# Feed-forward products in three 16-bit products, with downward products laced between upward ones

## The reference

```python
x = x + gnn(layernorm(x), src, dst, ...)
x = x + ffn(layernorm(x)[None], ...)[0]
# ffn: one batch of N = 6250 rows, D = 256, F = 512, E = 8 experts, 2 chosen for the whole batch
h   = gelu(einsum('nd,edf->enf', xf, W1) + b1[:, None, :], approximate=False)
y   = einsum('enf,efd->end', h, W2) + b2[:, None, :]
out = einsum('ne,end->nd', w_dense, y)          # w_dense: weights of the two chosen experts
out = layer_norm(out + x, gamma, beta)
```

## Time and profile before

| | |
|---|---|
| time, median of 3 runs | 3208.35 us (3207.71 to 3212.56) |
| the profiled execution | 3210.56 us, span of its trace 3208.6 us |
| PE busy | 3076.7 us (96%) |
| DVE busy | 1901.3 us (59%) |
| ACT busy | 855.9 us (27%) |
| POOL busy | 70.3 us (2%) |
| granted TensorE clock, mean | 0.975 of full speed |
| moved by DMA | 225.11 MB |

### The profile page before, as it was taken

How to read it: one execution, slowest core, us unless ns; L and a number is a source line. 1 busy time by engine, 2 the same in 40 slices (tenths; PEclk the granted TensorE clock), 3 DMA queues, 4 the chain that set the end, 5 groups by cost and what they waited for, 6 DMA issues and landing times.

```text
span 3208.6 us, 54202 instructions
## 1 busy us (share of the span) xinstructions
PE 3076.7 (96%) x17323; PEld 1804.0 (56%) x17323; DVE 1901.3 (59%) x5185; ACT 855.9 (27%) x1934; POOL 70.3 (2%) x168
## 2 busy tenths in 40 slices
PE   6999996999999999999999999999999999979998
PEld 4777773444444444444444444444444444468887
DVE  8999997555555545555554555555566666645554
ACT  4989896111111111111111111111111111132332
POOL 0000000000000000000000000000000000001010
PEclk9989996999999999999999999999999999989999
DMA  4323324122222222222222222222222222110000
GB/s 130 96 83 94 91 82 122 61 70 70 70 70 70 70 70 70 70 70 70 70 70 70 70 70 70 70 70 70 80 82 82 82 82 82 48 40 16 18 18 18
DMA packets 134110, 225.11 MB, mean 70 GB/s; under 512 B 12277, under 2 KB 106596, under 8 KB 134018
## 3 DMA queue, kind: packets, MB, share of 16 engines
q1 hardware_dynamic: 131666, 217.53, 20.9%
q0 software_dynamic: 2352, 6.40, 0.8%
HBM read 178.17 MB, written 45.74 MB: 70 GB/s over the span
## 4 chain that ended last, share of the span: by engine, by line
PE 84%; ACT 9%; DVE 3%; issue 2%; DMA 1%; SPq 0%; DVEq 0%; ACTq 0%; POOLq 0%; POOL 0%
PE bank L1416 64%; ACT tab L1094 7%; PE bank L1490 5%; PE bank L1496 5%; PE bank L1374 4%; PE bank L1364 1%; PE bank L1266 1%; PE bank L1286 1%; DVE later L757 1%; DMA tab<-in_x 1%; DVE region L724 1%; PE bank L1310 1%; ACT later L1118 0%; PE bank L1304 0%; ACT xnb L1112 0%
## 5 line engine op out<-in xcount | busy, mean ns | idle before, releaser
L1416 PE MATMUL bank<-tab,region 128*128 128x512 f16 x9604 | 2143.2, 380 | 14.3 <-DVE tab L840 14.0
L1416 PEld LDWEIGHTS bank<-tab,region 128*128 128x128 fp8e4 x9604 | 940.8, 98 | 1065.5 <-DVE tab L840 17.9
L1094 ACT ACTIVATE tab<-later 128x539 fp8e4<-128x539 uint8 x588 | 336.1, 674 | 1.9 <-DVE later L757 1.9
L724 DVE TENSOR_SCALAR region<-iota_w,src_col,src_w 128x540 bf16<-128x540 int16 x858 | 310.8, 415 | 0.4 <-issue 0.3
L941 DVE SCALAR_TENSOR_TENSOR region<-bank,c_back,later 128x256 f32<-128x256 f32 x196 | 94.8, 484 | 351.2 <-PE bank L1374 351.2
L1197 ACT ACTIVATE sd<-mv,eps_c 128x1 f32<-128x1 f32 x196 | 57.8, 295 | 817.6 <-DVE mv L948 817.6
L936 DVE TENSOR_TENSOR region<-bank,region 128x256 f16<-128x256 f32 x196 | 83.3, 425 | 287.7 <-ACT region L1193 287.7
L1193 ACT ACTIVATE region<-bank 128x256 f16<-128x256 f32 x196 | 75.3, 384 | 568.2 <-PE bank L1364 568.2
L1490 PE MATMUL bank<-tab 128*128 128x384 f32 (+1 forms) x544 | 178.0, 487 | 3.8 <-DMA b_s<-in_L_ffn_b 3.8
L1496 PE MATMUL bank<-tab 128*128 128x256 f32 (+1 forms) x784 | 175.5, 384 | 0.9 <-ACT tab L1221 0.9
L1490 PEld LDWEIGHTS bank<-tab 128*128 128x128 f32 x544 | 164.4, 310 | 13.4 <-issue 6.3
(11 more groups left out here) (199 smaller groups left out, 2232.8 us busy)
## 6 DMA issues: line engine op xcount, KB each, us to landing
region<-adjacency SPq DMA_DIRECT2D x196, 784.0 KB, 4.3
adjacency<-tab SPq DMA_DIRECT2D x12, 3136.0 KB, 13.7
region<-in_x POOLq DMA_DIRECT2D x48, 128.0 KB, 2.3
out<-region SPq DMA_DIRECT2D x48, 128.0 KB, 1.7
tab<-in_x SPq DMA_DIRECT2D x1, 6016.0 KB
tab<-in_L_ffn_W SPq DMA_DIRECT2D x4, 512.0 KB, 4.7
region<-in_L_gnn_Wl SPq DMA_DIRECT2D x1, 1024.0 KB, 5.4
later<-in_L_gnn_Wg SPq DMA_DIRECT2D x1, 1024.0 KB, 9.4
```

Of the source, the lines that this page charges most:

```text
L724: v.tensor_scalar(hot_s[:, j, :], iota_w[:, 0:WP], src_col[:, ds(first_block[0] + j, 1)], src_w[:, ds(first_block[0] + j, 1)], ALU.is_equa ...
L1094: ins = a.activation(stage[h][:, :, slot, f * LANES:f * LANES + n], counts[:, :, 0:n], ACT.Copy, saturate=False)
L1416: ins = mm(acc[a][:, :], A_s[:, a, m, :], tab[:, here + m, :], start=m == 0, stop=m == T - 1)
```

## The change

The same result is computed, with these edits:

- Every 32-bit operand of the feed-forward products is split into a scaled 16-bit high part (ACT, a copy with a scale) and a low part (DVE, `operand * scale - high`). Three 16-bit products (high x high, high x low, low x high) take the place of one 32-bit product. So W1, W2, the transposed tiles and Gelu's results are each split.
- The scales must bound the operands. Norms of every expert's weights come from a scan: POOL loads all of W1 and W2 in 32 pieces of [128, 512] by its own DMA queue, squares and sums them. It does this as soon as the first layer's table is ready, ahead of its loads of x. A small product, a root on ACT and a few small DVE steps turn the sums into scales ahead of the routing.
- PE's order is new: `down` of group i-1 and `turn` of group i+1, tile by tile, are laced between the upward slices 0-2, 3-5 and 6-7 of group i. `gx` (the split Gelu result) has two buffers for that. The loops are unrolled.
- The part `xf + b2c` (normalized tile and bias) and `H + fbet` are worked out ahead on POOL (`residuals`), two additions of 128x256 for each tile; the result on DVE becomes `gathered` (one fused operation, statistics) and `result` (two fused operations).
- The first expert's products wait for its own weights alone (`w1_in[a]`); the Gelu table is loaded ahead by a dummy operation.

```diff
+            def fetch(c):
+                if c > 1:
+                    pool.wait_ge(scan_done, c - 1)
...
+                    nc.gpsimd.dma_start(scan_s[c % 2].rearrange("p (e c) -> p e c", e=EX),
+                                        pieces[c]).then_inc(scan_in[c % 2], 16)
...
+            for c in range(len(pieces)):
+                fetch(c + 1)
+                m = sums[c // each]
+                hold(pool, scan_in[c % 2], (c // 2 + 1) * 16)
+                square(scan_s[c % 2])
+                if c:
+                    pool.wait_ge(scan_done, c)
+                nc.gpsimd.tensor_tensor(m, m, scan_s[c % 2].rearrange("p (e c) -> p e c", e=EX),
+                                        ALU.add).then_inc(scan_done, 1)
...
+            def residuals(t):
+                r = rows(t)
+                if t >= 3 * SUP:
+                    pool.wait_ge(y_taken, t - 3 * SUP + 1)
+                hold(pool, xf_ready, t + 1)
+                nc.gpsimd.tensor_tensor(xfb[0:r, t % (3 * SUP), :], xf_s[0:r, t % (2 * SUP), :], b2c[0:r, :],
+                                        ALU.add).then_inc(pre_done, 1)
+                nc.gpsimd.tensor_tensor(H[0:r, t, :], H[0:r, t, :], fbet[0:r, :], ALU.add).then_inc(pre_done, 1)
...
+            for i in range(GR + 1):
+                for u in range(SUP):
+                    if 0 <= (i - 1) * SUP + u < T:
+                        rsqrt((i - 1) * SUP + u)
+                    if (i + 2) * SUP + u < T:
+                        residuals((i + 2) * SUP + u)
```

DVE:

```diff
+            def xf_low(t):
+                i, u, r = t // SUP, t % SUP, rows(t)
+                dve.wait_ge(xfT_copied, t + 1)
+                v.scalar_tensor_tensor(out=xfT[:, i % 2, 1, :, u * P:u * P + r], in0=T3[3 + u % 2][:, :, 0:r],
+                                       scalar=ZSCALE, in1=xfT[:, i % 2, 0, :, u * P:u * P + r], op0=ALU.mult,
+                                       op1=ALU.subtract).then_inc(xfT_split, 1)
...
+            def g_low(i, f):
+                q, w = i * TOP * FC + f, in_group(i) * P if in_group(i) == SUP else LAST
+                dve.wait_ge(g_high, q + 1)
+                v.scalar_tensor_tensor(out=gx[:, i % 2, 1, f, 0:w], in0=gT[:, q % RING, 0:w],
+                                       scalar=g_scale[:, f // FC:f // FC + 1], in1=gx[:, i % 2, 0, f, 0:w], op0=ALU.mult,
+                                       op1=ALU.subtract).then_inc(g_split, 1)
...
-                own.done(v.tensor_tensor(Z[0:r], bank[5 + u][0:r, 0:D], b2c[0:r, :], ALU.add))
-                own.wait()
-                own.done(v.tensor_tensor(Zg[0:r], Z[0:r], Zn[0:r], ALU.add))
-                own.hold()
+                dve.wait_ge(pre_done, 2 * t + 1)
+                v.scalar_tensor_tensor(out=Zg[0:r], in0=bank[5 + u][0:r, 0:D], scalar=y_scale[0:r, :],
+                                       in1=xfb[0:r, t % (3 * SUP), :], op0=ALU.mult, op1=ALU.add).then_inc(y_taken, 1)
+                hold(dve, y_taken, t + 1)
...
-                own.done(v.tensor_scalar(Z[0:r], Zg[0:r], mv[0:r, 0:1], rs[0:r, :], ALU.subtract, ALU.mult))
...
-                own.done(v.tensor_tensor(Zn[0:r], Z[0:r], fgam[0:r, :], ALU.mult))
...
-                own.done(v.tensor_tensor(Zg[0:r], Zn[0:r], fbet[0:r, :], ALU.add))
...
+            def result(t):
+                i, u, r = t // SUP, t % SUP, rows(t)
+                dve.wait_ge(fvar_ready, t + 1)
+                own.done(v.scalar_tensor_tensor(out=Z[0:r], in0=Zg[0:r], scalar=mv[0:r, 0:1], in1=fgam[0:r, :],
+                                                      op0=ALU.subtract, op1=ALU.mult))
...
+                v.scalar_tensor_tensor(out=xb[0:r, u, :], in0=Z[0:r], scalar=rs[0:r, :], in1=H[0:r, t, :], op0=ALU.mult,
+                                       op1=ALU.add).then_inc(out_ready, 1)
...
+                mine(0)
+                mine(1)
+                if in_group(i - 2) == SUP:
+                    gathered((i - 1) * SUP - 1)
+                mine(2)
+                if in_group(i - 2) == SUP:
+                    result((i - 1) * SUP - 1)
+                before(0, gathered)
+                after(0)
+                mine(3)
+                before(0, result)
+                mine(4)
+                mine(5)
+                before(1, gathered)
+                after(1)
+                mine(6)
+                before(1, result)
+                mine(7)
+                after(2)
```

Here `mine(f)` is `g_low(i, f)`, `before(u, step)` a step of tile u of group i-1, and `after(u)` is `xf_low` of tile u of group i+1 and the normalization `xf` of tile u of group i+2. ACT and PE:

```diff
+                a.activation(gT[:, q % RING, 0:w], bank[q % RING][:, 0:w], ACT.Gelu, bias=b1_s[:, e, f % FC:f % FC + 1],
+                             scale=e_sel[:, e, 2:3]).then_inc(gelu_done, 1)
...
+                act.wait_ge(gelu_done, q + 1)
+                a.activation(gx[:, i % 2, 0, f, 0:w], gT[:, q % RING, 0:w], ACT.Copy,
+                             scale=g_scale[:, e:e + 1]).then_inc(g_high, 1)
...
+                for b, c in SPLIT:
+                    for k in range(KC):
+                        ins = mm(bank[q % RING][:, 0:w], W1x[:, b, f // FC * KC + k, f % FC:FF:FC], xfT[:, i % 2, c, k, 0:w],
+                                 start=n == 0, stop=n == 3 * KC - 1)
...
+                for f in range(TOP * FC):
+                    for b, c in SPLIT:
+                        ins = mm(bank[5 + u][0:r, 0:D], gx[:, i % 2, b, f, u * P:u * P + r], W2x[:, c, f // FC, f % FC, :],
+                                 start=n == 0, stop=n == 3 * TOP * FC - 1)
...
+            for i in range(GR + 1):
+                for u, part in enumerate(((0, 1, 2), (3, 4, 5), (6, 7))):
+                    if i < GR:
+                        for f in part:
+                            up(i, f)
+                    if u == SUP - 1 and u < in_group(i + 1):
+                        turn((i + 1) * SUP + u)
+                    if u < in_group(i - 1):
+                        down((i - 1) * SUP + u)
+                    if u < SUP - 1 and u < in_group(i + 1):
+                        turn((i + 1) * SUP + u)
```

More of the change, by code:

```diff
@@ new lines, in _ @@
+            for m in sums:
+                own.done(nc.gpsimd.memset(m, 0.0))
+            own.wait()
+            fetch(0)
+            for c in range(len(pieces)):
[7 more added lines that the diff above has]
+                                        ALU.add).then_inc(scan_done, 1)
@@ L601, in again @@
+            hold(pool, scan_done, len(pieces))
+            hold(pool, scan_in[0], (len(pieces) // 2 + 1) * 16)
+            for k, m in enumerate(sums):
+                total(m, width, e_lim[:, k * EX:(k + 1) * EX].unsqueeze(2))
+            square(scan_s[0][:, 0:EX * FC])
+            total(scan_s[0][:, 0:EX * FC].rearrange("p (e c) -> p e c", c=FC), FC, e_lim[:, 2 * EX:].unsqueeze(2))
+            own.wait()
+            pool.sem_inc(lim_set, 1)
             def again(t, i, u, r):
@@ new lines, in _, with w1_low @@
+            own.wait()
+            v.scalar_tensor_tensor(out=g_scale[:], in0=topw[:], scalar=e_most[:, 0:1], in1=e_sel[:, :, 4], op0=ALU.mult,
+                                   op1=ALU.mult).then_inc(g_scale_set, 1)
+            dve.wait_ge(g_scale_set, 1)
+            def w1_low(a):
+                for k in range(a * KC, (a + 1) * KC):
+                    dve.wait_ge(w1_high, k + 1)
+                    v.scalar_tensor_tensor(out=W1x[:, 1, k, :], in0=W1_s[:, k, :], scalar=e_sel[:, a, 0:1],
+                                           in1=W1x[:, 0, k, :], op0=ALU.mult, op1=ALU.subtract).then_inc(w1_split, 1)
@@ L1070, in _, with ffn, mine, before @@
-            result(T - 1, LOOP, 0, LAST)
+                xf(SUP + u)
+            w1_low(1)
+            dve.wait_ge(b2_in, 16 * TOP)
+            own.done(v.tensor_scalar(b2c[:], b2_s[:, 0, :], topw[:, 0:1], None, ALU.mult))
+            own.wait()
+            v.scalar_tensor_tensor(out=b2c[:], in0=b2_s[:, 1, :], scalar=topw[:, 1:2], in1=b2c[:],
+                                   op0=ALU.mult, op1=ALU.add).then_inc(ew_ready, 1)
+            def ffn(i):
+                def mine(f):
+                    if i < GR:
+                        g_low(i, f)
+                def before(u, step):
+                    if u < in_group(i - 1):
+                        step((i - 1) * SUP + u)
+                def after(u):
+                    if u < in_group(i + 1):
+                        xf_low((i + 1) * SUP + u)
+                    if u < in_group(i + 2):
+                        xf((i + 2) * SUP + u)
+                mine(0)
[17 more added lines that the diff above has]
+                after(2)
+                if i == 0:
+                    for a in range(TOP):
+                        w2_low(a)
@@ new lines, in w1_high_part, with w2_high_part @@
+            def w1_high_part(e):
+                act.wait_ge(sel_ready, e + 1)
+                act.wait_ge(w1_in[e], 32)
+                for k in range(e * KC, (e + 1) * KC):
+                    a.activation(W1x[:, 0, k, :], W1_s[:, k, :], ACT.Copy, scale=e_sel[:, e, 0:1]).then_inc(w1_high, 1)
+            def w2_high_part(e):
+                act.wait_ge(w2_in, 16 * TOP)
```

(15 more changed lines are left out.)

268 lines of the change are left out of this document (168 added, 100 removed).

## The result

| | before | after |
|---|---|---|
| time, median | 3208.03 us (3207.52 to 3212.56, 4 runs) | 3182.98 us (3174.37 to 3184.18, 4 runs) |
| span of the profiled execution | 3208.6 us | 3181.9 us |

The ratio is 0.9916, with a 95% interval of 0.9904 to 0.9928: 25 us faster, less than half of the 59 forecast. The time lies inside the range given (3113 to 3185), at its upper end.

What follows compares the result with a forecast made beforehand. PE's matrix work was taken to bound the last stage before, DVE's circle after. The stage's 63.9 us and its end's 1.3, less 6 for the scan, gave 59 us off 3208.35: 3149 us, range 3113 to 3185 (0.85).

Steps and rivals of the forecast that it cites:

- PE's costs: Last stage: 16-bit products of 256 columns at 0.108 us, stepped weight loads hidden; PE needs 16.3 us a group.
- rival 3: Last stage: PE's 256-column products take 0.146 us in long runs, not 0.108; 19.0 us a group, 3155 to 3160 us; chance 0.06.
- The last stage: First group 12.9 us, fifteen groups at 18.6, DVE closing the circle; 307.4 us against 371.3, 63.9 less.
- the milder rival: Last stage: PE's 1.5 us pause at a group's start halves the clock; some 1 us a group, 3165; 0.27 together with rival 2.
- POOL's additions: Last stage: six 128x256 additions a group at 0.67 us each, costing DVE 1.7 us a group.
- rival 2: Groups and scan: DVE pays fully for POOL's work; 19.3 us a group, 3168 us, 3180 with longest scan; 0.27 with the milder rival.
- The transition into the stage: Start of the last stage: first product waits for copies and lower parts of weights, 0 to 2.2 us later, 0.5 taken.
- The scan: First layer: POOL's 32 pieces lie in 13 to 20 tiles and cost 0 to 25 us, 6 taken.
- the slack: First layer: 0.66 us of DVE delay a tile is free before PE waits.
- full price: First layer: DVE pays at each collision, 0.38 us on average for 64 operations, 24 us before slack, at most 25.
- The sum: Whole kernel: 63.9 + 1.3 - 6 = 59 us less, 3149 us.

Runs made afterwards that it cites:

- The fills: Against the changed kernel, the scan left out and 128 POOL fills of 128x512 tiles (0.53 us each, reading nothing) in its place: 3141.28 us, ratio 0.9795.
- the two kernels with the moved pause: Changed kernel plus two one-element POOL powers per scan piece: between transfer issue and squaring 3160.59 us (0.9853), ahead of the issue 3183.32 us (0.9924).

## Why the prediction was wrong, point by point

- **PE's costs** held. 24 products of 256 columns start 2.62 us before what follows them (2963.60 to 2966.22 in the group shown), 0.109 each, against 0.108. The upward weights' step cost nothing; rival 3 is out.
- **The last stage** held in sum, a little better than said. The first group took 14.6 us (2872.39 to 2887.01) for a forecast 12.9, a whole group 18.26 (2887.01 to 3142.60, 14 of them) for 18.6, and the rest 35.0 from 3142.60 on, one group with it, for 18.6 + 18.3. From the first product to DVE's last operation that is 305.2 against a forecast 12.9 + 279 + 18.3 = 310.2. DVE is the closing circle, on the operation named. The pause ahead of each group did not cost clock, so the milder rival is out: the granted clock is 1.00 from 2950 to 3140 us.
- **POOL's additions** take 0.72 to 0.74 and 0.91 us in the group shown; I took 0.67. They add 18.30 - 16.60 = 1.7 us to a group by the kernel without them, and 1.7 was taken. That the two agree is in part luck. DVE paid 2.0 us a group, more than I took. But the group without additions is bound by PE at 16.60, where I had DVE close it at 16.8 and PE's work at 16.3. In the group shown 0.95 + 0.83 us stand for two operations of 0.48. Each DVE operation that meets an addition pays for what is left of it, as in rival 2. Only the result's operations met one: the lower parts, which rival 2 had counted in, take 607 ns beside the additions and 612 without.
- **The transition into the stage** cost 0.5 us, as taken: of the stage's start 44.0 us late, 43.5 were there at the end of the graph layers (DVE's last statistics, 2811.88 before and 2855.35 after).
- **The scan** is the step that failed: "0.38 us on average for each of 64 operations [...], 24 us less the slack, so 15, at most 25. In the middle: 6 us." It was 43. POOL's durations were near those taken (1.05 and 1.27 us for "say 1.0"). Three parts of the step were wrong. First, the arithmetic alone costs 24 us. The excess on DVE is 25.5 us or 0.40 for each of 64 operations, near the 0.38 taken, but the middle between 0 and full price had no ground, since POOL ran beside a DVE chain on which PE waits. The slack gave next to nothing back, because a piece took 3.7 us and not 4 to 7: the scan's arithmetic lay in some 6 tiles and not in 13 to 20, and 0.66 us in each is 4 us, not the 9 that were taken off. Where pauses spread the same arithmetic over 11 tiles, 25.2 us of excess cost only 14 to 16. Second, the squaring queued behind an issue adds 19 to 23 us (24 to 43 without a pause; 3160.6 to 3183.3 with it moved), which no row of before could show. Third, I counted only DVE's two-tile operations, while one-input ones were held too (294 to 1179 ns at L1053); with the arithmetic alone they are some 5 of the 25 us. So 0.38 came near with too few operations in it.
- **The sum** then is 70.63 - 43.96 = 26.7 us of span, where the 43.96 are the scan's 43.5 and the 0.5. With 43.5 for 6 the forecast would have been 3149 + 37.5 = 3186.5 us, 3.5 above the measured time.

Of the rivals, the second lies nearest by its time (3180 with the longest scan; its terms sum to 3178.5), but by another split: it had 19.3 us a group and at most 25 for the scan. So the range held the measured time by luck: no term in it went to 43 us for the scan, and a last stage slower than measured stood in for it.

What was held, and how, fits the port lock of the Trainium skill (page "SBUF — State Buffer", section "SBUF: two separate sides"). It names two kinds of DVE operation that exclude GpSimd: those in a two-port mode against any GpSimd operation, and those with two SBUF inputs only against one that reads SBUF. The fills agree with both halves, if the one-input TENSOR_SCALAR ran in such a mode (353 to 421 and 412 to 505 ns beside fills, 485 unchanged for two inputs); no run here shows the mode itself. The unchanged length of what reads a bank agrees too. That an operation waits for the whole instruction agrees with the ends 0.28 us behind POOL's. I had cited half of the rule, priced it as a rival for the groups, and in the sum cut the same price to a quarter for the scan. That a queued squaring holds DVE during the issue ahead of it rests on the two kernels with the moved pause and on the landing times above.

What stays open: how the hold begins during an issue. The traces show its bounds (from about 0.1 us behind the issue's start to the squaring's end), not its mechanism. Transfers issued without arithmetic behind them cost no time (3139.05 us); in that trace the excess over all of DVE's operations is 0.8 us. Of the 23 us between the two kernels with a moved pause, the excess of DVE's operations explains 15 (48.4 against 33.5); how the rest comes about no run shows.

## What to carry to other kernels

"The engine is idle there" does not make its time free: wide POOL arithmetic that reads SBUF held the wide elementwise DVE operations that read only SBUF until it ended. So price it at full overlap wherever DVE feeds the bound engine, or start it by a semaphore that DVE gives just before its own pause; here that one wait was worth 43 us, more than the change itself had gained. Keep a small operation between a transfer issued on POOL and arithmetic behind it (23 us here). And where a group closes on a chain over three engines, lacing independent products into the waits pays twice, since a long pause costs its length and then half clock: after 7.8 us without products the granted clock was 0.50, after the 1.7 to 1.8 us of the laced order it stayed 1.00.

## What the runs showed of the hardware that I had not expected

- A DVE operation of 0.43 us took up to 2.18 us when it started behind a transfer's issue (0.94 us) with a squaring queued straight after it.
- Of DVE's operations on SBUF alone the statistics were not held: 428 ns beside all of POOL's arithmetic. Nor were one-element reciprocals (164 ns), nor, with the arithmetic alone, the reductions of 128x512 (676 ns).
- On POOL, 128x512 elements took 1.05 us for a squaring, whose inputs are one tile, and 1.27 us for a sum of two tiles.
